# Gate and up projections as Strassen products of 2x2 blocks, the down projection with tokens stationary, and the first expert steps among the last attention pairs

## The chip, the cores and the metric

The kernel runs on one core of one Trainium2 chip. The metric is the device time of one execution in microseconds (us), the median of several runs. A core has five engines with an instruction stream each: TensorE (PE; its weight loads are listed apart as PEld), Vector (DVE), Scalar (ACT), GpSimd (POOL) and Sync (SP, which here issues all DMAs). They wait for each other by semaphores only. TensorE reads SBUF and writes PSUM; Vector and Scalar read both; GpSimd works on SBUF.

## What is computed

One transformer block on `x` (16 batches, 112 tokens, 256 channels: 1792 tokens). First cross attention to a context of 375 tokens per batch, then a mixture of 8 experts, each applied to every token, and summed with weights from two softmaxes over the experts:

```python
x = x + _L0_xattn_ref(_layernorm(x), ctx_1024, Wq, bq, Wk, bk, Wv, bv)
x = x + _L0_ffn_ref(_layernorm(x), w_router, w_gating, w_gate, w_up, w_down)
# ffn, with E, F = 8, 1024 and GATE_TEMP = 0.1
router_probs = softmax(x @ w_router); gate_weights = softmax(x @ w_gating / 0.1)
h = silu(einsum('bsh,ehf->ebsf', x, w_gate)) * einsum('bsh,ehf->ebsf', x, w_up)
expert_out = einsum('ebsf,efh->ebsh', h, w_down)
cw = router_probs * gate_weights; cw = cw / (sum(cw) + 1e-9)
out = einsum('ebsh,bse->bsh', expert_out, cw)
```

All is float32. The kernel reaches that with the faster matmul type fp32r in three passes: each operand is split into a high part (the value rounded to fp32r) and a low part (the value less the high part), and a product is high x high + high x low + low x high.

## The kernel before

**Streams.** Each engine's program is written out by hand, in order, in its own block (`@block.sync` L252, `gpsimd` L328, `scalar` L440, `vector` L633, `tensor` L902). An engine does its instructions in that order only; `wait_ge` on a semaphore holds everything behind it.

**Attention.** Batches go in 8 pairs of two. A pair is a chain through the engines: normalise (Scalar, `norm1`), transpose (TensorE), split into high (Scalar) and low parts (Vector), queries, scores, maxima (Vector, `maxima` L666), exponentials (Scalar), transposes of the probabilities, mix, values, residual, second layer norm (`stats2` L700 on Vector, `norm2_terms` L353 on GpSimd, `norm2` L448 on Scalar), transpose, router logits. Parts of neighbouring pairs are interleaved; `pair` in each block writes the order down. GpSimd makes the low part of the context (`low_ctx` L358, which on the profile's page shows as w_lo from shared, since the tiles overlap) and adds the value bias (`add_bv` L365). The transposed, normalised rows are split into `st_hi`, `st_lo` and copied by DMA into the SBUF tiles `h_in_hi`, `h_in_lo` (`keep_input` L276).

**Experts.** An expert's F = 1024 goes in two halves, a half in 4 tiles of 128 columns, the tokens in 4 chunks of 448. One step s (32 per expert) is one tile and one chunk. `gate_up` (L1074) makes 12 matmuls: weights (128 x 128) are the stationary side, 448 tokens the moving side, 2 slices of the 256 channels, 3 passes, for gate and for up. Scalar does Silu (`activate` L514), Vector multiplies with up (`hidden` L713, at L719), Scalar makes the high part (L522), Vector the low part (through `low`, L238). `down` (L1100) comes 2 steps later (LAG): 6 matmuls of 448 tokens, with the 128 x 128 tiles of `w_down` stationary. After 4 steps Vector multiplies the result with the combine weights, which lie along the tokens and were spread over the partitions by a DMA from DRAM (L871), and GpSimd adds it to `acc` (L420). At the end `acc` is transposed back (`sum_rows` L1142) and added to x. Weights come by DMA, half by half; Scalar makes high parts (L511), GpSimd low parts (L378).

**Overlap of the stages.** The first 8 steps of expert 0 lie among the last attention chain (from `pair` 7 on) by hand. Loops: the middle attention pairs and experts 1 to 6 are hardware loops. All matmuls of three passes are recorded at L233, inside `accumulate`.

Of the kernel before, what the change touches and what calls it, by code (L numbers as in the profile page):

```python
# [5 lines left out]
def xattn_ffn_kernel(nc, x, ctx, wq, bq, wk, bk, wv, bv, w_router, w_gating, w_gate, w_up, w_down, out):  # L16
# [3 lines left out]
    B, TQ, D = x.shape  # L20
# [10 lines left out]
    CH = 4  # L31
    TC = T // CH
    BC = B // CH
    HALVES = 2
    FH = F // HALVES
    FT = FH // P
    STEPS = HALVES * CH * FT
    LAG = 2
    HS = 4
    EARLY = 2 * FT  # L40
# [4 lines left out]

    x_v = x.rearrange("b q d -> q b d")
    out_v = out.rearrange("b q d -> q b d")
    ctx_v = ctx.rearrange("(n two) (p t) d -> n p two (t d)", two=2, t=KT)
    gate_v = w_gate.rearrange("e (k p) (h f) -> e h p k f", p=P, h=HALVES)
    up_v = w_up.rearrange("e (k p) (h f) -> e h p k f", p=P, h=HALVES)  # L50
    down_v = w_down.rearrange("e (h t p) d -> e h p t d", p=P, h=HALVES)
    cw_dram = nc.dram_tensor("cw_dram", (E, T), fp32).ap()

    es = ExitStack()
    with es:
# [6 lines left out]
        def at_least(engine, semaphore, count):  # L62

            if not isinstance(count, int) or count > 0:
                engine.wait_ge(semaphore, count)

# [14 lines left out]
        m_hi = sb("m_hi", [P, DK, D], fp32r)  # L81
        m_lo = sb("m_lo", [P, DK, D], fp32r)
        wv_hi = sb("wv_hi", [P, DK, D], fp32r)
        wv_lo = sb("wv_lo", [P, DK, D], fp32r)
        wr_raw = sb("wr_raw", [P, DK, 2 * E])
        wr_split = sb("wr_split", [P, DK, 2, 2 * E], fp32r)
        wr_hi, wr_lo = wr_split[:, :, 0, :], wr_split[:, :, 1, :]

        xs = sb("xs", [TQ, B, D])
        h_in_hi = sb("h_in_hi", [P, DK, T], fp32r)  # L90
        h_in_lo = sb("h_in_lo", [P, DK, T], fp32r)
        w_raw = sb("w_raw", [P, 3, DK * FH])
        w_hi = sb("w_hi", [P, HALVES, 3, DK * FH], fp32r)
        w_lo = sb("w_lo", [P, HALVES, 3, DK * FH], fp32r)


        cn_hi, cn_lo = [w[0:KP, HALVES - 1, :, :].rearrange("p a n -> p (a n)")[:, 0:4 * KT * D]
                        .rearrange("p (s b t d) -> p s b t d", s=2, b=2, t=KT) for w in (w_hi, w_lo)]
        ct_hi = sb("ct_hi", [P, 2, DK, SK], fp32r)
        ct_lo = sb("ct_lo", [P, 2, DK, SK], fp32r)  # L100
        shared = sb("shared", [P, 4 * KT * D])
        ctx_raw = shared[0:KP, :].rearrange("p (s b n) -> p s b n", s=2, b=2)
        xt_hi = sb("xt_hi", [P, DK, TP], fp32r)
# [119 lines left out]
        def inside(p):  # L223

            return not isinstance(p, int) or 0 <= p < PAIRS
# [1008 lines left out]
```

## Time and profile before

| | us |
|---|---|
| median of 3 runs | 1077.63 |
| lowest, highest | 1076.79, 1095.28 |
| span of the profiled execution | 1092.8 |
| TensorE busy in it | 1066.6 |
| Vector, Scalar, GpSimd busy | 515.0, 420.8, 315.2 |

The profile is of one execution, which took 1.4% longer than the median of the runs. Lines such as L233 are lines of the kernel. A row of the timeline gives start and duration in us; neighbouring instructions of one kind are merged (x6). "[2.41 <-DMA ...]" is the idle time of the engine before it and what ended it. A matmul's duration covers its way through the array, so matmuls overlap and what one costs is the distance between two starts.

### The profile page before, as it was taken

What the parts mean: (1) busy time and instruction counts of PE and PEld (TensorE: products, weight loads), DVE (VectorE), ACT (ScalarE), POOL (GpSimd) and SP (SyncE); (2) the same over time, 40 slices, a digit from 0 to 9 for tenths busy, and PEclk for the clock granted to TensorE, in tenths of its full rate; (3) what the DMA queues carried; (4) which work ended last, traced back from release to release, by engine and by line L of the source; (5) the groups of instructions that cost most, each with busy time, mean ns of one, the idle gap of its engine ahead of it and who ended that gap; (6) DMA issues with size and microseconds to landing.
All of it is one profiled execution on the core that took longest, in us unless ns stands there. A gap on an engine that the chain in (4) does not pass through costs nothing.

```text
span 1092.8 us, 14974 instructions
## 1 busy us (share of the span) xinstructions
PE 1066.6 (98%) x5457; PEld 975.0 (89%) x5457; DVE 515.0 (47%) x832; ACT 420.8 (39%) x787; POOL 315.2 (29%) x247
## 2 busy tenths in 40 slices
PE   6798999999999999999999999999999999999998
PEld 5688999999999999999999999999999999999997
DVE  5777754434444343434443444434344444344444
ACT  3677644424342332434243424333243434243322
POOL 3554403304132131414141413213141413141110
PEclk8899999999999999999999999999999999999999
DMA  7223212100102010101010010201010201000001
GB/s 178 94 79 99 96 37 92 62 14 18 57 1 75 17 58 0 66 17 66 0 53 21 17 58 0 74 13 61 0 66 17 66 0 44 31 17 1 1 17 51
DMA packets 34086, 47.38 MB, mean 43 GB/s; under 512 B 3016, under 2 KB 23864, under 8 KB 34056
## 3 DMA queue, kind: packets, MB, share of 16 engines
q1 hardware_dynamic: 34056, 46.97, 13.6%
q8 instruction: 19, 0.31, 0.1%
q14 instruction: 11, 0.09, 0.0%
HBM read 41.40 MB, written 1.89 MB: 40 GB/s over the span
## 4 chain that ended last, share of the span: by engine, by line
PE 91%; DMA 3%; DVE 2%; POOL 1%; issue 1%; ACT 1%; SPq 0%; DVEq 0%; POOLq 0%
PE ps L233 89%; DMA shared<-in_ctx 3%; POOL w_lo L362 1%; DVE part L662 0%; POOL rstd L347 0%; DVE neg_top L676 0%; PE ps L1150 0%; PE ps L997 0%; PE ps L920 0%; PE ps L946 0%; POOL xs L370 0%; DVE top L669 0%; DVE top_all L674 0%; DVE bn L637 0%; PE ps L991 0%
## 5 line engine op out<-in xcount | busy, mean ns | idle before, releaser
L233 PE MATMUL ps<-h_in_hi,w_hi 128*128 128x448 f32 x1024 | 377.4, 369 | 0.0
L233 PE MATMUL ps<-h_in_lo,w_hi 128*128 128x448 f32 x1024 | 376.7, 368 | 0.0
L233 PE MATMUL ps<-h_in_hi,w_lo 128*128 128x448 f32 x1024 | 375.5, 367 | 0.0
L719 DVE TENSOR_TENSOR hid<-act,ps 128x448 f32<-128x448 f32 x256 | 159.0, 621 | 365.3 <-PE ps L233 294.3
L420 POOL TENSOR_TENSOR acc<-acc,part 128x896 f32<-128x896 f32 x59 | 125.1, 2121 | 636.8 <-DVE part L871 636.8
L233 PE MATMUL ps<-hs,w_hi 128*128 128x448 f32 x1008 | 288.2, 366 | 0.0
L522 ACT CAST hs<-hid 128x448 fp32r<-128x448 f32 x256 | 145.2, 567 | 348.4 <-DVE hid L719 348.4
L238 DVE TENSOR_TENSOR hs<-hid,hs 128x448 fp32r<-128x448 f32 x256 | 185.6, 725 | 162.1 <-ACT hs L522 162.1
L519 ACT ACTIVATE act<-ps 128x448 f32<-128x448 f32 x256 | 139.6, 545 | 260.5 <-PE ps L233 260.3
L233 PEld LDWEIGHTS ps<-h_in_hi,w_lo 128*128 128x128 f32 x1024 | 192.3, 188 | 19.0
L233 PEld LDWEIGHTS ps<-h_in_hi,w_hi 128*128 128x128 f32 x1024 | 192.4, 188 | 18.8
L233 PEld LDWEIGHTS ps<-h_in_lo,w_hi 128*128 128x128 f32 x1024 | 192.1, 188 | 17.7
L233 PEld LDWEIGHTS ps<-hs,w_hi 128*128 128x128 f32 x1008 | 188.6, 187 | 19.4 <-issue 0.2
L233 PE MATMUL ps<-hs,w_lo 128*128 128x448 f32 x504 | 185.1, 367 | 0.0
L378 POOL TENSOR_TENSOR w_lo<-w_raw,w_hi 128x512 fp32r<-128x512 f32 x96 | 132.6, 1413 | 53.6 <-ACT w_hi L511 53.6
L233 PEld LDWEIGHTS ps<-hs,w_lo 128*128 128x128 f32 x504 | 94.3, 187 | 8.5
L871 DVE TENSOR_TENSOR part<-ps,shared 128x896 f32<-128x896 f32 x59 | 64.0, 1084 | 0.0
L511 ACT CAST w_hi<-w_raw 128x512 fp32r<-128x512 f32 x96 | 51.7, 618 | 0.0
L362 POOL TENSOR_TENSOR w_lo<-shared,w_hi 125x768 fp32r<-125x768 f32 (+1 forms) x16 | 29.0, 1835 | 3.7 <-ACT w_hi L502 3.4
L920 PE MATMUL ps<-ident,shared 125*128 125x125 f32 x96 | 15.1, 300 | 10.0 <-DMA shared<-in_ctx 10.0
L920 PEld LDWEIGHTS ps<-ident,shared 125*128 125x128 f32 x96 | 12.3, 156 | 11.9 <-issue 6.2
L345 POOL TENSOR_TENSOR var<-mv,eps_c 112x2 f32<-112x2 f32 (+2 forms) x12 | 2.4, 198 | 67.1 <-DVE mv L706 52.7
(140 smaller groups left out, 582.8 us busy)
## 6 DMA issues: line engine op xcount, KB each, us to landing
w_raw<-in_L_ffn_w_gate SPq DMA_DIRECT2D x16, 512.0 KB, 3.6
w_raw<-in_L_ffn_w_up SPq DMA_DIRECT2D x16, 512.0 KB, 4.7
w_raw<-in_L_ffn_w_down SPq DMA_DIRECT2D x16, 512.0 KB, 5.6
shared<-cw_dram SPq DMA_DIRECT2D x32, 224.0 KB, 3.2
shared<-in_ctx SPq DMA_DIRECT2D x8, 750.0 KB
h_in_hi<-st_hi SPq DMA_DIRECT2D x8, 224.0 KB, 3.0
h_in_lo<-st_lo SPq DMA_DIRECT2D x8, 224.0 KB, 3.4
out_dram<-xs SPq DMA_DIRECT2D x3, 448.0 KB, 3.2
```

Of the source, the lines that this page charges most:

```text
L233: ins = nc.tensor.matmul(dst, w, m, start=first and i == 0, stop=last and i == len(passes) - 1)
L238: return nc.vector.tensor_tensor(dst, src, high.bitcast(fp32), ALU.subtract)
L345: nc.gpsimd.tensor_tensor(var, mv[:, :, 1], eps_c[:, 0:n], ALU.add).then_inc(norm_step, 1)
L362: nc.gpsimd.tensor_tensor(cn_lo[:, bass.ds(p % 2, 1), b, :, :], ctx_raw[:, bass.ds(p % 2, 1), b, :].rearrange("p s (t d) -> p s t d", t=KT ...
L378: ins = nc.gpsimd.tensor_tensor(w_lo[:, half, i, s], w_raw[:, i, s], w_hi[:, half, i, s].bitcast(fp32), ALU.subtract)
L420: nc.gpsimd.tensor_tensor(a, a, part[:, c % 2, :, :], ALU.add).then_inc(acc_done, 1)
L511: ins = nc.scalar.copy(w_hi[:, half, i, s], w_raw[:, i, s])
L519: nc.scalar.activation(act[:, s % 2, :], ps_g[s % 2], ACT.Silu).then_inc(act_done, 1)
L522: nc.scalar.copy(hs[:, 0, s % HS, :], hid[:, s % 2, :]).then_inc(hid_hi_done, 1)
L719: nc.vector.tensor_tensor(hid[:, s % 2, :], act[:, s % 2, :], ps_u[s % 2], ALU.mult).then_inc(hid_done, 1)
L871: nc.vector.tensor_tensor(dst, ps_d[c % 2], cw_all[:, None, c * TC:(c + 1) * TC].broadcast_to((P, DK, TC)), ALU.mult).then_inc(part_done, 1)
L920: ins = nc.tensor.transpose(ps_c[:, k, t * KP:(t + 1) * KP], ctx_raw[:, slot, b, at:at + P], ident[0:KP, 0:KP])
```

## The change

**Strassen products.** Tokens go in two halves (CP = 2) of 896, each in two chunks of TC = 448. A *quad* is two neighbouring tiles of F, the two slices of the 256 channels, and the two chunks of a half: a product of 2x2 blocks by 2x2 blocks. It needed 8 block products and takes 7, from sums of the input blocks (`xc`, made once per token half) and of the weight blocks. The 64 quads n cover everything; two quads (FPAIRS) make a *group* g, the half of an expert's F for one token half. Each of the 7 products is three passes, as before:

```diff
+    PRODUCTS = {1: (A11, B11), 2: (A12, B21), 3: (S4, B22), 4: (A22, T4), 5: (S1, T1), 6: (S2, T2), 7: (S3, T3)}
+            def product(n, m, p, bank, first):
+                cp, fp = n // FPAIRS % CP, n % FPAIRS
+                a, b = PRODUCTS[p]
+                return accumulate(bank, three(w_hi[:, fp, m, b, :], w_lo[:, fp, m, b, :], xc_hi[:, cp, a, :], xc_lo[:, cp, a, :]),
+                                  first=first, onto=not first)
+            def gate_2_7(n):
+                pe.wait_ge(gate_p1, n + 1)
+                product(n, 0, 2, g_a, False).then_inc(gate_prod, 1)
+                pe.wait_ge(gate_sum, 5 * n + U2_SUM)
+                product(n, 0, 7, g_x, False).then_inc(gate_prod, 1)
```

`gate_1_6_5` starts three PSUM banks, `gate_2_7` adds products 2 and 7 onto two of them, `gate_4_3` products 4 and 3; the same for up. Between them Scalar copies product 1 out (`gate_first`, `up_first`) and Vector makes five sums for gate and five for up, each from PSUM and an SBUF tile, in place:

```diff
+            def gate_first(n):
+                at_least(sc, hid_done, 4 * (n - 1) + HID21)
+                first_product(n, gate_prod, g21, g_a, gate_p1)
+            def up_first(n):
+                at_least(sc, hid_lo_done, 4 * (n - 1) + HID21)
+                first_product(n, up_prod, u21, u_a, up_p1)
+            def up_u2(n):
+                ve.wait_ge(up_p1, n + 1)
+                ve.wait_ge(up_prod, 7 * n + PROD[6])
+                at_least(ve, hid_lo_done, 4 * n)
+                nc.vector.tensor_tensor(u12, u_x, u21, ALU.add).then_inc(up_sum, 1)
```

Each tile is there once. The four hidden blocks of a quad (`hidden11`, `22`, `21`, `12`) are products of Silu(gate) and up; only `hidden11` reads PSUM, the other three read two SBUF tiles. Scalar makes their high parts (`high_hidden`), GpSimd their low parts, which Vector did before.

**Weights.** A *set* is gate and up for one pair of tiles. GpSimd makes four sums of 128 x 256 (`sums_of_set`), Scalar one high copy of 128 x 1792 (`high_set`), GpSimd one low part of 128 x 1792 (`low_set`); `w_down` is split in one piece of 1024 columns (`high_down`, `low_down`).

**Down with tokens stationary.** For each group and each of its 7 token tiles of 128, 12 matmuls with the hidden tokens as the stationary side and 256 channels moving. The result lies with tokens on partitions, so the combine weight is a number per partition and one Vector instruction scales and adds it (`add_rows`). No broadcast of `cw` by DMA, no `acc` addition on GpSimd, no `sum_rows`. The rows after attention go to DRAM (`keep_x1`) and come back as 14 tiles of 128 tokens, which is the accumulator.

```diff
+            def row_passes(g, i, fp):
+                return [t for j in range(2) for t in three(h[:, 0, j, toks], h[:, 1, j, toks],
+                                                           w[:, 0, 2 * fp + 1 - j, :], w[:, 1, 2 * fp + 1 - j, :])]
+            def add_rows(g, i, src):
+                nc.vector.scalar_tensor_tensor(acc[:, tile, :], src, cw[:, tile, e:e + 1], acc[:, tile, :],
+                                               ALU.mult, ALU.add).then_inc(acc_done, 1)
```

**The order** of the steady stretch, on TensorE, Vector, Scalar and GpSimd:

```diff
+            def quad(n):
+                g = n // FPAIRS - 1
+                gate_1_6_5(n)
+                if n % FPAIRS:
+                    down(g, 4)
+                up_1_6_5(n)
+                if n % FPAIRS:
+                    down(g, 5)
+                gate_2_7(n)
+                up_2_7(n)
+                down(g, 6 if n % FPAIRS else 0)
+                gate_4_3(n)
+                if n % FPAIRS == 0:
+                    down(g, 1)
+                up_4_3(n)
+                if n % FPAIRS == 0:
+                    down(g, 2)
+                    down(g, 3)
...
+                if n > 1:
+                    gate_u2(n)
+                    if odd:
+                        add_rows(g, 2, ps_r[2])
+                        add_rows(g, 3, ps_r[3])
+                    up_u2(n)
+                gate_u3_c22(n)
+                if n > 1 and odd:
+                    add_rows(g, 4, ps_r[4])
+                    add_rows(g, 5, ps_r[5])
+                up_u3_c22(n)
...
+                if n > 1 and odd:
+                    add_rows(g, 6, ps_r[6])
+                gate_c21_c12(n)
+                hidden11(n)
+                if n > 1 and not odd:
+                    add_rows(g, 0, ps_r[0])
+                    add_rows(g, 1, ps_r[1])
+                hidden22(n)
+                up_c21(n)
+                up_c12(n)
+                hidden21(n)
+                hidden12(n)
...
+                    gate_first(n)
+                    high_hidden(n - 1, HID21, u21, 0, TC)
+                    high_hidden(n - 1, HID12, u12, 1, 0)
+                    up_first(n)
...
+                    low_hidden(n - 1, HID21, u21, 0, TC)
+                    low_hidden(n - 1, HID12, u12, 1, 0)
...
+                low_hidden(n, HID11, g11, 0, 0)
+                low_hidden(n, HID22, u22, 1, TC)
```

Scalar's `high_set` comes after `up_first` in the first and last of four quads; GpSimd's `low_set`, `sums_of_set` and `low_down` come between its two pairs of low parts.

**The first steps.** Quads 0 and 1 lie among the last attention pairs. The input sums of token half 0 are made in pairs 6 and 7 (Vector `sums_1_3`, `sums_2_4`; Scalar `high_comb`; GpSimd `low_comb`), those of half 1 after the last pair:

```diff
+            last = PAIRS - 1
+            transpose_probs(last, 0)
+            transpose_probs(last, 1)
+            gate_4_3(0)
+            mix_ctx(last)
+            up_1_6_5(0)
+            transpose_mix(last)
+            up_2_7(0)
+            values(last)
+            transpose_norm2(last - 1)
+            up_4_3(0)
+            gate_1_6_5(1)
+            transpose_norm2(last)
+            up_1_6_5(1)
+            route(1)
+            gate_2_7(1)
+            up_2_7(1)
+            gate_4_3(1)
+            up_4_3(1)
```

The router is two plain float32 matmuls for each of 14 token tiles, in two calls (`route(0)` in pair 6, `route(1)` above), instead of split ones for each pair. The weight split of sets 0 and 1 lies in pairs 1 to 4. Nothing is a hardware loop any more: every instruction is written out.

## Rows read from the trace of the kernel before

**Rows 1.** The page, busy us (share of the span) and instructions of each engine
```profile
PE 1066.6 (98%) x5457; PEld 975.0 (89%) x5457; DVE 515.0 (47%) x832; ACT 420.8 (39%) x787; POOL 315.2 (29%) x247
```
**Rows 2.** The chain that ended last in order of time: start, us, what
```profile
161.78 879.73 PE ps L233 x4272
1041.51 0.87 PE ps L1150 x8
```
**Rows 3.** Groups by line: out<-in, shapes, count | busy us, mean ns | idle before, releaser
```profile
L238 DVE TENSOR_TENSOR hs<-hid,hs 128x448 fp32r<-128x448 f32 x256 | 185.6, 725 | 162.1 <-ACT hs L522 162.1
L719 DVE TENSOR_TENSOR hid<-act,ps 128x448 f32<-128x448 f32 x256 | 159.0, 621 | 365.3 <-PE ps L233 294.3 <-ACT act L519 70.9
...
L378 POOL TENSOR_TENSOR w_lo<-w_raw,w_hi 128x512 fp32r<-128x512 f32 x96 | 132.6, 1413 | 53.6 <-ACT w_hi L511 53.6
L420 POOL TENSOR_TENSOR acc<-acc,part 128x896 f32<-128x896 f32 x59 | 125.1, 2121 | 636.8 <-DVE part L871 636.8
...
L519 ACT ACT_TABLE_LOAD x2 | 2.6, 1283 | 0.0
```
**Rows 4.** Timeline of PE: start us, us, what; same matmul, one expert step apart
```profile
603.96 0.37 PE L233 MATMUL ps<-h_in_hi,w_hi 128*128 128x448 f32 x1
...
607.67 0.37 PE L233 MATMUL ps<-h_in_hi,w_hi 128*128 128x448 f32 x1
```
**Rows 5.** Timeline and chain: first and last of 18, of 10; router; plain fp32
```profile
137.62 0.28 PE L233 MATMUL ps<-w_hi,pt_hi 125*112 125x256 f32 x1
...
139.63 0.28 PE L233 MATMUL ps<-w_hi,pt_lo 125*112 125x256 f32 x1
...
104.92 0.28 PE L233 MATMUL ps<-xt_hi,m_lo 128*128 128x224 f32 x1
...
105.93 0.27 PE L233 MATMUL ps<-xt_hi,m_lo 128*128 128x224 f32 x1
...
107.83 0.09 PE ps L991
...
37.16 3.55 PE L997 MATMUL ps<-lg 112*112 112x256 f32 x8
```
**Rows 6.** Windows: length, busy of PE, PEld, DVE, ACT, POOL, clock, DMA, GB/s
```profile
120.00:140.00 20.00, 19.98 (x134) 18.78 (x134) 13.78 (x28) 11.72 (x24) 4.91 (x6) 1.00 0.12 40
...
200.00:620.00 420.00, 420.00 (x2041) 382.56 (x2040) 182.57 (x255) 150.37 (x275) 118.09 (x71) 1.00 0.11 35
```
**Rows 7.** Timeline of DVE and POOL, alone and beside each other
```profile
129.06 0.62 DVE L238 TENSOR_TENSOR at_lo<-ps,at_hi 128x448 fp32r<-128x448 f32 x1 [2.01 <-ACT at_hi L489]
129.60 0.61 DVE L238 TENSOR_TENSOR st_lo<-ps,st_hi 128x448 fp32r<-128x448 f32 x1
...
43.63 3.79 POOL L378 TENSOR_TENSOR w_lo<-w_raw,w_hi 128x512 fp32r<-128x512 f32 x3 [7.69 <-ACT w_hi L511]
...
123.12 3.66 POOL L362 TENSOR_TENSOR w_lo<-shared,w_hi 125x768 fp32r<-125x768 f32 x2
...
123.84 2.95 DVE L674 SCALAR_TENSOR_TENSOR top_all<-q_bk,c,top 112x2 f32<-112x2 f32 x1
...
619.23 8.30 POOL L378 TENSOR_TENSOR w_lo<-w_raw,w_hi 128x512 fp32r<-128x512 f32 x6
```
**Rows 8.** Timeline of PE after three idles, and the window of 40 to 60
```profile
53.38 0.34 PE L233 MATMUL ps<-wv_hi,at_hi 128*112 128x256 f32 x1 [4.27 <-DVE at_lo L238]
...
72.21 0.86 PE L920 MATMUL ps<-ident,shared 125*128 125x125 f32 x6 [2.41 <-DMA shared<-in_ctx]
...
73.08 0.33 PE L233 MATMUL ps<-ct_lo,q_hi 128*112 128x376 f32 x1
...
97.77 0.85 PE L920 MATMUL ps<-ident,shared 125*128 125x125 f32 x6 [2.21 <-DMA shared<-in_ctx]
...
98.72 0.52 PE L233 MATMUL ps<-ct_lo,q_hi 128*112 128x376 f32 x1
...
40.00:60.00 20.00, 15.44 (x107) 14.71 (x107) 16.86 (x42) 13.07 (x27) 11.40 (x13) 0.90 0.12 44
```

More of the change, by code:

```diff
@@ new lines, in xattn_ffn_kernel @@
+        ctx_raw = shared[0:KP, 0:4 * KT * D].rearrange("p (s b n) -> p s b n", s=2, b=2)
+        gate_t = shared[:, 0:4 * TC].rearrange("p (s t) -> p s t", s=4)
+        up_t = shared[:, 4 * TC:7 * TC].rearrange("p (s t) -> p s t", s=3)
+        g21, g12, g22, g11 = [gate_t[:, i, :] for i in range(4)]
+        u21, u12, u22 = [up_t[:, i, :] for i in range(3)]
+        CT, PT, CN = 2 * DK * SK, 2 * KT * TQ, 4 * KT * D
+        sizes = [CT, CT] + [DK * TP] * 6 + [DK * D] * 4 + [PT, PT, CN, CN]
+        starts = [sum(sizes[:i]) for i in range(len(sizes) + 1)]
@@ L434, in _ @@
-            expert(0, first=True)
-            with pool.Fori(1, E - 1) as e:
-                expert(e)
-            expert(E - 1, last=True)
+            low_set(0)
+            pair(3)
+            sums_of_set(1)
+            pair(4)
+            low_set(1)
+            pair(5)
+            low_comb(0, COMB_SPLITS[0:3])
+            pair(6)
+            low_comb(0, COMB_SPLITS[3:4])
+            pair(7)
+            norm2_terms(6)
+            low_hidden(0, HID11, g11, 0, 0)
+            low_hidden(0, HID22, u22, 1, TC)
@@ L440, in _ @@
+            for n in range(1, QUADS):
+                quad(n)
+            low_hidden(QUADS - 1, HID21, u21, 0, TC)
+            low_hidden(QUADS - 1, HID12, u12, 1, 0)
         @block.scalar
@@ L633, in _ @@
+            for n in range(1, QUADS):
+                quad(n)
+            high_hidden(QUADS - 1, HID21, u21, 0, TC)
+            high_hidden(QUADS - 1, HID12, u12, 1, 0)
         @block.vector
@@ L828, in _ @@
+            stats2(last)
+            hidden22(0)
+            up_c21(0)
+            hidden21(0)
+            up_c12(0)
+            hidden12(0)
+            sums_1_3(1)
+            gate_u2(1)
+            up_u2(1)
+            sums_2_4(1)
+            keep_logits(1)
+            lv = logits[:, :, :].rearrange("p i (two e) -> p (i two) e", two=2)
+            ve.wait_ge(logits_done, CP)
             nc.vector.tensor_reduce(lg_top[:], lv, AX.X, ALU.max).then_inc(cw_step, 1)
             ve.wait_ge(cw_step, 1)
-            nc.vector.tensor_tensor(lg[:], lv, lg_top[:, :, None].broadcast_to((TQ, 2 * B, E)), ALU.subtract).then_inc(cw_step, 1)
@@ L902, in _ @@
+            for n in range(1, QUADS):
+                quad(n)
+            for i in range(RT):
+                add_rows(GROUPS - 1, i, ps_end[i])
         @block.tensor
@@ new lines, in _ @@
+            for n in range(2, QUADS):
+                quad(n)
+            g = GROUPS - 1
+            pe.wait_ge(wd_done, SETS)
+            pe.wait_ge(hid_lo_done, 4 * (QUADS - 1))
+            pe.wait_ge(acc_done, RT * g)
+            pe.wait_ge(act_done, 4 * (QUADS - 1) + HID11)
+            pe.wait_ge(gate_sum, 5 * QUADS)
+            for i in range(RT):
+                accumulate(ps_end[i], row_passes(g, i, 0), first=i % 2 == 0, last=False)
+            pe.wait_ge(hid_lo_done, 4 * QUADS)
```

995 lines of the change are left out of this document (491 added, 504 removed).

## The prediction

> **What bounds the kernel now.** I read the page's busy row first [rows 1], then the chain of work that ended last [rows 2], then the groups by line [rows 3]. TensorE is busy for 1066.6 of 1092.8 us. One piece of the chain, from 161.8 to 1041.5 us, is matmuls of L233 and nothing else: 880 us in which TensorE waits for nobody. Before it the attention pairs take about 121 us, with some TensorE waits, and after it come 51 us more of the same with four transposes of sums. Vector is idle for 365 us before L719 alone, and GpSimd for 637 us before L420 [rows 3]. So a matmul taken away is worth its own spacing, as long as nothing else becomes late.
>
> A matmul lasts 0.37 us and overlaps the next, so the price is the distance of starts: 18 matmuls of 448 columns in 3.71 us, 0.206 each [rows 4]. With 256 columns it is 17 in 2.01 us, 0.118 each [rows 5]. There the stationary side has 112 columns and after the change 128; 224 columns with 128 stationary ones come every 0.112 [rows 5], so the wider load is hidden under 0.118.
>
> **What TensorE does less.** Before: 8 experts x 32 steps x 18 = 4608 matmuls of 448 columns, 949 us. After: 64 quads (two 128-column tiles of F by 896 tokens) x 2 x 7 products x 3 passes = 2688 of 448 columns, 553.5 us, and 32 groups x 7 token tiles x 12 = 2688 of 256 columns, 317 us. Sum 870.5. Gain 78.5. The down projection has the same columns as before; all of the gain is the eighth of gate and up. The four `sum_rows` go, 0.87 each, 3.5 [rows 2]. The router turns from 64 fp32r matmuls of 0.09 (L991, [rows 5]) into 28 of plain fp32. Bounds: 0.09 each, and 0.42 each (8 of 256 columns in 3.55 us, [rows 5]); that is -3.5 to +5.5. I take 0.21 a piece, no change. The x1 round trip over DRAM, the `cw` broadcasts that go, and the smaller weight loads lie under TensorE work: DMA engines are 11% busy there [rows 6]. SP issues the accumulator load behind `load_down(0)` and `load_set(2)`, after the last `transpose_norm2`; Vector first needs it in quad 2, some 20 us later. If it is late, `add_rows` and all sums queued behind it on Vector wait (the start rival below).
>
> **What the other engines do more, for one group (two quads, 84 + 84 matmuls, 27.2 us of TensorE).** Vector: 28 operations of 448 columns (20 sums, 8 products) and 7 row additions. One begins 0.54 after the one before it (129.06, 129.60, [rows 7]), a row addition between 0.31 (by its 256 columns) and 0.54, and I take 0.4: 18 us. Scalar: 20 copies or Silus of 0.57 and its part of the splits, about 14. GpSimd: 3 pieces of 512 took 3.79 us [rows 7], one of 896 2.12 [rows 3], so 2.2 ns a column: 448 columns 1.12, 1792 columns 4.1, and with 8 low parts, a `low_set`, a `sums_of_set` and half a `low_down` 17 us a group, against 7.6 us in as much time now (118 of 420, [rows 6]). None is over 27, so no engine becomes the bound by its sum. The question is the order, since each product waits for a sum on Vector, and the tiles g21, u21, u12 hold both the next first product and the last hidden block.
>
> Laid beside each other, with t=0 at gate P1 of an even quad: the gate P7 of the odd quad before landed at -4.9 (18 products, 3.7, and down 6, 1.4, follow it, less 0.16 of landing). Vector then has 10 operations of 0.54, two waits of 0.12 for its own result and 3 rows of 0.4: `hidden21` begins at 1.9 and is done at 2.6. Scalar makes the gate's P1 copy first, then the high part: 3.7. GpSimd does `low21` to 4.8 and `low12` to 5.95. The U2 sum of up waits for all four low parts (`hid_lo_done`): 6.0 to 6.6. TensorE can start up P7 at 6.7; 27 matmuls of 0.206 bring it there at 5.56. **Late by 1.2 us, once a group.** Late next would be gate P7 by 0.1. In odd quads the two downs of 1.4 each in between cover the same chain, and in the last part of an even quad downs 1 to 3 do. I take 1.3 x 31 groups = 40.
>
> Here a shared thing matters. Vector operations with two SBUF inputs stretch while GpSimd works, and those that read PSUM don't: two elements took 2.95 us at 123.84, when GpSimd had begun two pieces at 123.12 that ended at 126.78; the low parts of L238 take 725 ns in the mean [rows 3] against 620 for the PSUM kind [rows 7]. `hidden22`, `hidden21`, `hidden12` and the input sums are of that kind. But the handover overlaps: 6 GpSimd pieces took 8.30 us at 619 [rows 7] against 6 x 1.26 = 7.58; three low parts of L238 fall among them (one in each step of 3.71), 0.24 for each and not 0.62. My 1.2 counts it so. Counted in full, `low22` starts only behind `hidden12` (3.4), the low parts end at 6.75 and P7 starts at 7.5: 2.0 late.
>
> The Trainium skill (SBUF — State Buffer, "SBUF: two separate sides") calls this pair of ports an exclusive lock that the first of the two holds for its whole instruction, while the other fully blocks. By that rule the sum would be 22 us higher than mine; the rows at 619 to 628 bear out the blocking, and speak for less than the whole instruction.
>
> **Where the first steps lie.** TensorE hardly waits in the last pairs now: 19.98 of 20 us busy from 120 to 140 [rows 6]. The same layout from pair 6 on, with the durations of [rows 3, 7], gives these waits after the change. (a) In pair 6 GpSimd gets three pieces of `low_comb` (2.1 + 1.1 + 2.1) ahead of `norm2_terms(4)`, and they wait for Scalar's copies; `transpose_norm2(4)` comes 3.2 late. (b) Eight short ones in pairs 6 and 7 (a comb part 1.1, the copy of P1 behind two exponentials 1.3, others under 0.8): 5.3. (c) `gate_4_3(0)` waits for U3 behind residual, statistics and two low parts on Vector: 2.1; up P7(0): 1.4. (d) `transpose_norm2(7)`: statistics are done late, and `norm2_terms(7)` is queued on GpSimd behind a low part: 4.3. (e) `gate_4_3(1)`: Vector stands in `sums_2_4(1)` until GpSimd has `low_comb` done, and `gate_u3_c22(1)` is queued behind it: 4.7. (f) Quad 2 waits for Scalar's two table loads (1283 ns, [rows 3]) and for the combine weights on Vector: 5.5. Sum 26.5. Bounds: 12, if (d) and (e) shrink to the short ones; 35, if (a) and (e) meet GpSimd at its loaded rate. Before pair 6 the weight split moves (7.6 us of GpSimd go, 13.8 come, some late); TensorE waited 4.3 us up to 53.4 for it, and 2.2 up to 97.8 for a context load [rows 8]. I take 0, bounds -4 to +4.
>
> After both idles matmuls were slower for a while: one of 376 columns lasted 0.52 at 98.7 and not 0.33 as at 73.1; the granted clock over 40 to 60 us is 0.90 [rows 5, 8], which is 4 us of the 20 at 1.2 GHz and not 2.4, most of them at work: about 1.6 us lost each time. (a), (d) and (e) are as long: 5.
>
> **The sum:** 1092.8 - 78.5 - 3.5 + 40 + 26.5 + 5 + 0 = 1082. The profiled execution is 1.4% over the median shown (1077.63), so 1082 x 0.986 = 1067. The saving shrinks with a faster execution while the waits on Vector and GpSimd do not, so I say **1068**.
>
> **Rivals.**
> - *The chain stays hidden* (20%). If sums, copies and low parts answer as fast as matmuls need them, only the start costs: 1042, so about 1027. For it: Vector 18 of 27 us, Scalar 14 of 27. Against it: the layout above, with starts of 0.54 that several rows show.
> - *GpSimd's row is the loop, the other sign* (20%). One mechanism: the low parts. At the port held in full it is 2.0 a group: 1103, so 1088. If GpSimd works at its present mean (512 columns in 1413 ns, not 1263, [rows 3]) and Vector misses its turn as at 123.84 [rows 7], the low parts grow by 12%, at each of four and at the 4.1 us piece, and a group is 2.9 late: 1131, so 1115. It is slower than before from 1.65 a group, by over 2% from 2.35.
> - *The clock falls in the steady stretch* (8%). An idle of 1.2 to 2.0 us once a group; 2.4 us up to 72.2 were not followed by slower matmuls (376 columns in 0.33 at 73.1), 2.2 up to 97.8 were (0.52 at 98.7) [rows 8]. 31 x 1.6 = 50 more: 1132, so 1116.
> - *A start far worse than laid out* (5%): weights or the accumulator land late, GpSimd stands in `sums_of_set`: +25, 1092.
> - The forecast: 47%, its own range 1048 to 1088.
>
> **How the numbers follow.** "Within 2%" is 1056 to 1099, about what a measurement of this kernel can tell from no change. Faster: the first rival, and the fifth of the forecast under 1056, 0.30. Slower: half of the second, the clock, and a little of the start, 0.21. Same: 0.49. The range leaves out the lower half of the first rival and the upper ends of second and third: 1032 to 1108.
>
> **What would show it.** Spacing 0.206 and 0.118 in the steady stretch, or the term 78.5 is wrong. A wait of TensorE in L233 of 1.2 to 2 us in total once in about 28.5 us, ended by Vector or Scalar, and none in odd quads; a period of 27.2 is the first rival. `hidden` operations of two SBUF inputs over 0.62 in the mean, sums with PSUM at 0.62. Waits of 3 to 5 us near 120, 160 and 173 us. The granted clock at 1.00 from 190 us on. GpSimd busy at about 60%. The prediction is wrong if Vector or GpSimd has a larger sum than 18 and 17 us a group, or if the waits before quad 3 sum to under 10.

## The result, and the profile after

The changed kernel takes 1100.24 us (median of 4 runs, 1099.99 to 1101.56) against 1077.21 us for the kernel before: a ratio of 1.0219, 95% interval 1.0199 to 1.0239. It is slower by 23 us (the interval leaves open whether by more or less than 2%), where I forecast 1068 with a range of 1032 to 1108. One thing has to be said to read the numbers: the kernel before has executions of two lengths, about 1077 and about 1096 us, and the profile shown above is of one of the long ones; the ratio is against the short ones.

The page of the changed kernel, busy us of each engine, against [rows 1]:

```profile
PE 1021.7 (93%) x6160; PEld 941.5 (86%) x6160; DVE 789.0 (72%) x1361; ACT 499.1 (45%) x874; POOL 643.7 (59%) x532
```

TensorE is busy 45 us less than before, and the span is 7 us longer. So 52 us of idle have come. Its windows (length, busy of PE, PEld, DVE, ACT, POOL, granted clock, DMA) show that they lie in two places. Up to 194 us, where quad 2 has just begun, it is idle for 44 us at a clock of 0.83; in the steady stretch it is idle for 6.6 us in 200:

```profile
0.00:194.00 194.00, 150.03 (x878) 138.05 (x879) 126.32 (x268) 106.19 (x207) 98.05 (x121) 0.83 0.27 82
...
200.00:400.00 200.00, 193.41 (x1171) 178.15 (x1169) 146.72 (x243) 89.55 (x151) 123.90 (x92) 1.00 0.10 30
```

**The steady stretch.** The chain of waits, one group (28.8 us) like the next; this is the turn from an odd to an even quad, and gate P1 of the even quad starts at 393.47:

```profile
395.34 0.81 DVE shared L856
...
396.17 0.02 ACT shared L567
...
396.60 0.58 ACT arena L594
...
397.25 2.51 POOL arena L411 x2
...
399.87 0.64 DVE shared L827
...
400.55 1.46 PE ps L248 x8
```

It is the chain of the forecast, link by link: `hidden21` (L856), Scalar's copy of gate P1 (L567), the high part (L594), `low21` and `low12` (L411), the U2 sum of up (L827), up P7. TensorE's timeline over it (start, us, the idle before it and what ended it):

```profile
397.52 0.36 PE L248 MATMUL ps<-xc_hi,w_lo 128*128 128x448 f32 x1
398.45 0.47 PE L248 MATMUL ps<-xc_hi,w_hi 128*128 128x448 f32 x1 [0.57 <-DVE shared L807]
398.76 0.36 PE L248 MATMUL ps<-xc_lo,w_hi 128*128 128x448 f32 x1
...
400.55 0.47 PE L248 MATMUL ps<-xc_hi,w_hi 128*128 128x448 f32 x1 [0.43 <-DVE shared L827]
```

The idle shown is 0.57 and 0.43, but by starts gate P7 comes 0.73 later than a spacing of 0.2, up P7 0.59, and the first matmul behind each pause takes 0.31 to the next and not 0.20. Together it is 1.75 us a group; 84 matmuls at 0.2027 and 84 at 0.1196 (12 in 1.44) make 27.07, and the period is 28.82.

**The start.** TensorE's longer waits, against 2.4 us and less after 55 us in [rows 8]:

```profile
88.38 1.01 PE L1099 MATMUL ps<-ident,early 112*128 112x112 f32 x4 [2.40 <-ACT early L489]
...
125.54 1.01 PE L1099 MATMUL ps<-ident,early 112*128 112x112 f32 x4 [3.48 <-ACT early L489]
...
170.80 1.01 PE L1099 MATMUL ps<-ident,early 112*128 112x112 f32 x4 [4.60 <-ACT early L489]
...
187.36 0.44 PE L248 MATMUL ps<-xc_hi,w_hi 128*128 128x448 f32 x1 [0.18 <-ACT shared L583]
...
191.32 0.74 PE L248 MATMUL ps<-xc_hi,w_hi 128*128 128x448 f32 x1 [3.11 <-DVE shared L819]
```

The last two rows are gate P1 and gate P6 of quad 2. P6 goes to a PSUM bank that a gate sum of quad 1 reads, and waits for all of them; the last two (L817, L819) stand on Vector behind the combine weights, which end at 190.2. In experiments 4 and 12 I took this wait for one before gate P3 of quad 1. That product starts at 185.19, without a wait.

The first of the waits, at 88.38, is one that I had not laid out. L1099 is `transpose_norm2`. It waits for Scalar's `norm2`, that for GpSimd's `norm2_terms(2)`, and GpSimd stood in `sums_of_set(1)` in front of it, since the weights were late (timeline of GpSimd):

```profile
82.76 0.74 POOL L390 TENSOR_TENSOR w_raw<-w_raw 128x256 f32<-128x256 f32 x1 [9.63 <-DMA w_raw<-in_L_ffn_w_up]
```

SP issues `load_set(1)` behind `load_ctx(5)`, which waits for the low part of pair 3's context; so its two DMAs were issued at 72.3 and 72.8, and the second landed at 82.7.

### The profile page after: what moved, and what is told of

It reads as the page before. It is cut to its first block, busy times and chain, and to the rows that moved or that the text cites. A ratio compares the mean times of both kernels' runs of the same rounds, so it can differ in the third digit from the quotient of the medians.

```text
span 1099.8 us, 16297 instructions
## 1 busy us (share of the span) xinstructions
PE 1021.7 (93%) x6160; PEld 941.5 (86%) x6160; DVE 789.0 (72%) x1361; ACT 499.1 (45%) x874; POOL 643.7 (59%) x532
## 4 chain that ended last, share of the span: by engine, by line
PE 53%; DVE 24%; POOL 10%; issue 4%; ACT 4%; DMA 4%; DVEq 0%; SPq 0%; POOLq 0%; ACTq 0%
PE ps L248 51%; POOL arena L411 7%; DVE xsacc L867 3%; DMA shared<-in_ctx 3%; DVE shared L856 2%; DVE shared L811 2%; DVE shared L833 2%; DVE shared L827 2%; DVE shared L813 2%; DVE shared L819 2%; ACT arena L594 2%; DVE shared L831 2%; DVE shared L846 2%; DVE shared L851 2%; DVE shared L837 1%
## 5 line engine op out<-in xcount | busy, mean ns | idle before, releaser
L411 POOL TENSOR_TENSOR arena<-shared,arena 128x448 fp32r<-128x448 f32 x256 | 311.7, 1233 | 309.1 <-ACT arena L594 306.2
L248 PE MATMUL ps<-arena 128*128 128x256 f32 (+4 forms) x3120 | 425.3, 289 | 7.8 <-DVE arena L252 5.5
L248 PEld LDWEIGHTS ps<-arena 128*128 128x128 f32 (+2 forms) x3120 | 414.4, 194 | 15.0 <-DVE arena L252 4.5
L248 PE MATMUL ps<-xc_hi,w_hi 128*128 128x448 f32 x896 | 342.0, 382 | 38.0 <-DVE shared L807 17.1
L248 PE MATMUL ps<-xc_lo,w_hi 128*128 128x448 f32 x896 | 329.8, 368 | 0.0
L248 PE MATMUL ps<-xc_hi,w_lo 128*128 128x448 f32 x896 | 329.8, 368 | 0.0
L248 PEld LDWEIGHTS ps<-xc_hi,w_hi 128*128 128x128 f32 x896 | 170.9, 191 | 80.3 <-DVE shared L807 28.2
L248 PEld LDWEIGHTS ps<-xc_hi,w_lo 128*128 128x128 f32 x896 | 170.3, 190 | 14.4
L248 PEld LDWEIGHTS ps<-xc_lo,w_hi 128*128 128x128 f32 x896 | 171.2, 191 | 9.0
L594 ACT CAST arena<-shared 128x448 fp32r<-128x448 f32 x256 | 141.1, 567 | 75.6 <-DVE shared L851 55.4
L567 ACT COPY shared<-ps 128x448 f32<-128x448 f32 x128 | 68.3, 533 | 172.4 <-PE ps L248 121.5
L827 DVE TENSOR_TENSOR shared<-ps,shared 128x448 f32<-128x448 f32 x64 | 40.0, 624 | 105.1 <-ACT shared L567 59.2
L867 DVE SCALAR_TENSOR_TENSOR xsacc<-ps,cw,xsacc 128x256 f32<-128x256 f32 x224 | 98.6, 476 | 13.8 <-PE ps L248 13.8
L861 DVE TENSOR_TENSOR shared<-shared 128x448 f32<-128x448 f32 x64 | 70.2, 1097 | 0.1
L856 DVE TENSOR_TENSOR shared<-shared 128x448 f32<-128x448 f32 x64 | 67.3, 1051 | 0.1
L851 DVE TENSOR_TENSOR shared<-shared 128x448 f32<-128x448 f32 x64 | 58.7, 917 | 0.0
```

What stands on the lines that cost most here:

```text
L248: ins = nc.tensor.matmul(dst, w, m, start=first and i == 0, stop=last and i == len(passes) - 1, skip_group_check=onto)
L411: nc.gpsimd.tensor_tensor(h[:, 1, j, at:at + TC], tile, h[:, 0, j, at:at + TC].bitcast(fp32), ALU.subtract).then_inc(hid_lo_done, 1)
L567: nc.scalar.copy(dst, bank).then_inc(done, 1)
L594: nc.scalar.copy(hs[n % HSLOTS][:, 0, j, at:at + TC], tile).then_inc(hid_hi_done, 1)
L827: nc.vector.tensor_tensor(u12, u_x, u21, ALU.add).then_inc(up_sum, 1)
L851: nc.vector.tensor_tensor(u22, g22, u22, ALU.mult).then_inc(hid_done, 1)
```

## The experiments

Experiments 5 and 9 look at the kernel before again; all others are edits of the changed kernel (1100.2 us). They were made in three groups. The kernel before, beside them, took 1077.03 us in the first four, 1077.74 in the next four and 1079.02 in the last four (medians of its short executions), so a difference of 1 to 2 us between two groups says nothing.

**1. Work of TensorE in front of the two late products.** The half of the first four row tiles that needs only the earlier quad's hidden blocks comes ahead of gate P7.

```diff
+            def down_early(g, some):
+                for i in some:
...
+                    accumulate(ps_r[i], row_passes(g, i, 0), first=i % 2 == 0, last=False)
...
                     down(g, 4)
+                else:
+                    down_early(g, (0, 1))
                 up_1_6_5(n)
...
                     down(g, 5)
+                else:
+                    down_early(g, (2, 3))
                 gate_2_7(n)
```

> The changed kernel with one thing moved: in every even quad, the 6 matmuls of each of the first four row tiles whose stationary side is the hidden block of the earlier quad of the group (24 matmuls of 256 columns, 2.87 us) come before gate P7, the other 6 of each stay where they were. Nothing else is moved. Theory A (in an even quad TensorE waits only because gate P7 and up P7 come before Vector and GpSimd have closed the last quad, 1.75 us a group): the need for both comes 2.87 us later, the waits of 0.6 and 0.4 us at gate P7 and up P7 vanish, a group goes from 28.8 to about 27.1 us, and the time falls by about 53, to 1047 us. Theory B (Vector and GpSimd go round in a loop of their own that is as long as 28.8 us): the wait comes back later in the same quad, which has 12 matmuls less behind its P7 products, and the time stays within 10 us of 1100.

Measured: 1047.27 us (ratio 0.9729, 0.9712 to 0.9745), 53 us less, as theory A had it. The chain of waits of this kernel has one piece from 300 us on:

```profile
299.88 724.70 PE ps L248 x4500
```

So Vector and GpSimd have no loop of their own of 28.8 us. They were late by a fixed amount in even quads, and 2.9 us of work in front of the need covers it.

**2. A second set of tiles.** g21, g12, u21, u12 of odd quads lie elsewhere, and the waits on their low parts go back by one quad.

```diff
-                at_least(sc, hid_lo_done, 4 * (n - 1) + HID21)
-                first_product(n, up_prod, u21, u_a, up_p1)
+                at_least(sc, hid_lo_done, 4 * (n - 2 if n > 2 else n - 1) + HID21)
+                first_product(n, up_prod, buf(n, U21), u_a, up_p1)
```

> The changed kernel with a second set of the tiles g21, g12, u21, u12 for odd quads (in the tile of the input sums, which is free by then). A first product or a U2 sum then waits for no high or low part of the quad before; only Vector's own queue is left. Theory A (the low parts hold up P7: hidden21, Scalar, two low parts, U2): the wait before up P7 vanishes, the one before gate P7, which hangs on Vector being through with hidden12, stays at 0.6 to 0.9; 0.9 us a group less, 28 us in all: 1072 us. Rival (the port is held by four low parts in a row, and Vector's own ten operations are what comes late): the wait moves and no more than 8 us are gained, 1092 or more.

Measured: 1064.79 us (0.9886, 0.9870 to 0.9903), 35 us less where 28 were expected and the rival allowed 8. TensorE has no wait before up P7 any more and one of 0.36 before gate P7. About 1.15 of the 1.75 us were the reuse of a tile; the rest is at gate P7, which waits for Vector's U2 sum of gate.

**3. GpSimd's order in the attention pairs.**

```diff
             pair(3)
-            sums_of_set(1)
             pair(4)
-            low_set(1)
+            sums_of_set(1)
             pair(5)
-            low_comb(0, COMB_SPLITS[0:3])
+            low_set(1)
```

In pairs 6 and 7 the low parts of the input sums follow `norm2_terms`.

> The changed kernel with GpSimd's order in pairs 3 to 7 changed alone: the sums of weight set 1 come after the work of pair 4 instead of ahead of it, the low part of set 1 after pair 5, and the low parts of the input sums after the terms of the second layer norm in pairs 6 and 7 instead of ahead of them. Theory A (the lost time before quad 2 is instructions that stand in GpSimd's queue, waiting for a DMA or for Scalar, ahead of norm2_terms): TensorE's waits of 2.4 us at 88 and 3.5 us at 125 vanish, the granted clock between 80 and 140 us rises from 0.83 to over 0.9, and the time falls by 8 to 14 us, to about 1090. Rival (the context's DMA and Scalar's longer queue set the pairs): 3 us or less.

Measured: 1093.41 us (1.0155, 1.0138 to 1.0172), 6.8 us less; the waits at 88 and 125 are gone and the clock from 60 to 100 us is 1.00 (0.91 and 0.83 in the changed kernel). From 100 to 140 us it is 0.83 (0.91 and 0.83), and there waits of 4.9 and 4.2 us came up before `values`, where Vector is late. One reason for the first is in the timeline of Vector and GpSimd:

```profile
95.20 1.24 POOL L373 TENSOR_TENSOR xsacc<-xsacc,early 112x256 f32<-112x256 f32 x2
95.30 5.09 DVE L759 SCALAR_TENSOR_TENSOR neg_top<-q_bk,c,top_all 112x2 f32<-112x2 f32 x1
...
96.39 3.98 POOL L400 TENSOR_TENSOR w_lo<-w_raw,w_hi 128x1792 fp32r<-128x1792 f32 x1
```

A Vector operation on two elements a partition, from two SBUF inputs, takes 5.09 us, until GpSimd has ended two short instructions and the long low part of a weight set. The exponentials, queries and scores of the pair hang on it.

**4. Matmuls for nothing in the waits.**

```diff
+            def fill_wait(n):
+                for _ in range(n):
+                    nc.tensor.matmul(ps[0:TQ, 7, 448:512], ident[:, 0:TQ], ident[:, 0:64], start=True, stop=True)
```

> The changed kernel with matmuls whose result nobody reads, put where TensorE waits: 16 before transpose_norm2(4) (a wait of 3.5 us), 20 before transpose_norm2(7) (4.6 us), 14 before gate P3 of quad 1 (3.1 us). Each is plain fp32 of 64 columns. No wait is removed. Theory A (a good part of what the start costs is not the waits but the slow matmuls after them, at granted clocks of 0.74 to 0.75 from 140 to 200 us): the clock there rises and the time falls by 4 to 10 us. Rival (the slow matmuls lie beside waits for other engines and cost nothing themselves): the time stays within 2 us, or rises by as much as the dummies overshoot.

Measured: 1100.89 us (1.0222, 1.0200 to 1.0244): no change. The window of 160 to 180 us of the changed kernel, and then of this one:

```profile
160.00:180.00 20.00, 14.92 (x72) 13.91 (x72) 12.23 (x20) 7.90 (x15) 11.03 (x11) 0.75 0.37 119
```

```profile
160.00:180.00 20.00, 18.66 (x126) 17.30 (x124) 13.11 (x19) 7.11 (x13) 12.37 (x11) 0.91 0.45 144
```

The clock rose from 0.75 to 0.91. Behind the router TensorE was 5.7 us earlier than in the changed kernel (175.14 against 180.82), and half of that was waited away at gate P4 of quad 1, for Vector:

```profile
182.19 0.51 PE L248 MATMUL ps<-xc_hi,w_hi 128*128 128x448 f32 x1 [2.81 <-DVE shared L811]
```

So at the end of the attention most of the slow matmuls lie beside Vector's queue, as the rival has it. But 2.4 us were left (182.19 against 184.59), and the experiment does not say what they are worth: the third group of matmuls stood before gate P3 of quad 1, where the changed kernel has no wait, and took 5.1 us. In the steady stretch TensorE was 1.1 us earlier than in the changed kernel (224.48 against 225.54 for the first gate P7 that waits), which the times of the two kernels don't tell apart.

**5 and 9. The kernel before, profiled again.**

> The kernel before, unchanged, for a second profile. In the profile of 1092.8 us matmuls of 448 columns are 0.2059 us apart for most of the steady stretch; in the changed kernel and its variants they are 0.2027 apart, with and without waits. Theory A (the 1.4% between that execution and the median is this spacing, so it belongs to the execution and not to the kernel, and must not be taken off the changed kernel's sum): an execution of about 1077 shows 0.2025 to 0.203 throughout. Rival (the spacing is a property of the kernel, as its matmuls follow each other without a break; the 16 us lie in the attention pairs): 0.2059 again, and the pairs are shorter.

> The kernel before, unchanged, once more: the second profile was again of an execution of 1097 us, with 448 columns 0.2059 apart, and of 7 executions beside it 4 took 1077.7 to 1078.1 and 3 took 1096 to 1097. If this profile is of an execution of about 1077: Theory A (the two times are two matmul spacings) expects 0.2023 to 0.203 through the steady stretch, 4608 matmuls by 0.0035 being the 16 us; the rival expects 0.2059 and the difference elsewhere. If it is of 1096 again, nothing is told apart.

The first of these executions took 1097.34 us and showed 0.2059 again. The second took 1077.10. Its chain has the piece of [rows 2] with the same 4272 matmuls, 862.34 us and not 879.73:

```profile
162.08 862.34 PE ps L233 x4272
```

That is 0.2019 a matmul and not 0.2059; the 17.4 us are nearly all of the 17.7 between the two spans (1075.1 and 1092.8), and up to 162 us the two agree within 0.3. Theory A holds. The changed kernel's own matmuls are 0.2027 apart in its profile. Why an execution takes one spacing or the other stays open; the granted clock is 1.00 in both.

**6. The first two quads behind the attention.** Quads 0 and 1 begin when the last pair is through, on all engines.

```diff
-            gate_4_3(0)
             mix_ctx(last)
-            up_1_6_5(0)
             transpose_mix(last)
-            up_2_7(0)
             values(last)
...
+            route(1)
+            gate_1_6_5(0)
+            up_1_6_5(0)
```

> The changed kernel with quads 0 and 1 taken out of the last attention pairs: the last pair's attention runs to its end, then quad 0 begins. The steady stretch is untouched. Theory A (the quads among the last pairs fill waits that the attention chain has anyway): the chain of the last pair then stands open, some 10 to 15 us of waits come, and the 17 us of work of quads 0 and 1 lie behind it: 1110 to 1120 us. Rival (the quads themselves make the waits, through Scalar's and GpSimd's queues, as in transpose_norm2(7) behind a low part): the time stays within 5 us of 1100.

Measured: 1114.05 us (1.0335, 1.0311 to 1.0358), 14 us more. Theory A: that part of the change is worth having, since the waits of the attention chain are there with or without the quads. `transpose_norm2(7)` waits 4.7 us here too.

**7. Short pieces.** Experiment 3, with the low parts of sets 0 and 1 in 4 instructions each.

> The kernel with GpSimd's order changed (1093.4 us), and in it the low parts of weight sets 0 and 1, which lie among the attention pairs, in 4 pieces of 384 and 512 columns each instead of one of 1792 (3.98 us). There a Vector operation of two elements took 5.09 us beside it. Theory A (Vector waits for the end of a GpSimd instruction, so long instructions hurt its short ones): that operation takes 1 to 2.5 us, and the time falls by 2 to 4 us, to 1090. Rival (Vector gets no turn between GpSimd's pieces either): no change, within 1 us.

Measured: 1094.98 us (1.0161, 1.0138 to 1.0184), which is no gain. The same small operation of Vector still takes 4.56 us, over two short GpSimd instructions and three of the four pieces:

```profile
100.20 4.56 DVE L766 SCALAR_TENSOR_TENSOR neg_top<-q_bk,c,top_all 112x2 f32<-112x2 f32 x1
...
100.11 1.24 POOL L373 TENSOR_TENSOR xsacc<-xsacc,early 112x256 f32<-112x256 f32 x2
101.30 4.39 POOL L403 TENSOR_TENSOR w_lo<-w_raw,w_hi 128x512 fp32r<-128x512 f32 x4
```

No gain, as the rival has it: between GpSimd instructions that follow each other at once, Vector got no turn at about 101.3, 102.4 and 103.5, and one at 104.6. It is not so each time. In experiment 3, beside three pieces that follow each other as closely, two such operations took 1.07 and 1.05 us:

```profile
111.71 1.07 DVE L757 SCALAR_TENSOR_TENSOR top_all<-q_bk,c,top 112x2 f32<-112x2 f32 x1
112.82 1.05 DVE L759 SCALAR_TENSOR_TENSOR neg_top<-q_bk,c,top_all 112x2 f32<-112x2 f32 x1
...
110.64 5.24 POOL L380 TENSOR_TENSOR xc_lo<-xf,xc_hi 128x896 fp32r<-128x896 f32 x3 [1.78 <-ACT xc_hi L551]
```

By the lengths of these pieces (2.1 and 1.1 us) each operation ended about where a piece did, near 112.7 and 113.8. What decides between the two cases stays open.

**8. All of it together,** with Vector's `sums_2_4(0)` behind `at_low(5)`.

> The changed kernel with the row matmuls moved, the second set of tiles, GpSimd's order and the short pieces all together, and Vector's second pair of input sums after at_low of pair 5 instead of ahead of it. The parts that act on different stretches should add: 1047.3 less 6.8 (GpSimd's order), less 2 to 4 (pieces), less 2 to 4 (the wait of 4.2 us before values(5), where Vector stood in the sums): 1032 to 1037 us. The second tiles add nothing, as no wait is left for them. Rival (the waits of the start only move): 1040 or more.

Measured: 1039.95 us (0.9652, 0.9630 to 0.9674). Against experiment 1 that is 7.3 less, which is GpSimd's order alone (6.8); the pieces and Vector's order added nothing that can be told. Closer to the rival. That the waits of the start only moved, as it says, was not tried part by part.

**10 and 11. One more GpSimd operation of 448 columns ahead of `low21`,** in odd quads, then in even quads.

```diff
                 if n > 1:
+                    if n > 2 and n % 2 == 1:    # == 0 in experiment 11
+                        pool.wait_ge(hid_hi_done, 4 * (n - 1) + HID21)
+                        nc.gpsimd.tensor_tensor(xf[:, 0, :], u21, hs[(n - 1) % HSLOTS][:, 0, 0, TC:2 * TC].bitcast(fp32), ALU.subtract)
                     low_hidden(n - 1, HID21, u21, 0, TC)
```

> The changed kernel with one more GpSimd operation of 448 columns (1.25 us) ahead of low21 in every odd quad from 3 on, whose result nobody reads. In an odd quad two row tiles (2.9 us) lie before gate P7, and the U2 sum of up is done 3.1 us before up P7 needs it. Theory A (the low-part chain is late in even quads only): within 3 us of 1100. Rival (GpSimd's total, 58% busy and holding the port, is what slows the loop): +15 to +37 us.

> The same additional GpSimd operation, but in every even quad from 4 on, 30 in all. Theory A (in even quads hidden21, Scalar, low21, low12, U2, up P7 is the path): each delays up P7 by its own 1.25 us, 30 x 1.25 = 37: about 1137 us. Rival (the wait at gate P7, which hangs on Vector's queue, sets the quad, and up P7 merely follows): less than 15 us.

Measured: 1099.45 us in odd quads (1.0191, 1.0154 to 1.0227), and 1155.71 in even quads (1.0707, 1.0654 to 1.0760). So the chain decides in even quads only, as laid out. But there it costs 55 us, not 37: 1.8 us for each 1.25. TensorE now waits already at up P2, for Scalar's copy of up P1, which waits for `low21`. The timeline of TensorE in the kernel with the even ones has the rest:

```profile
716.38 0.47 PE L248 MATMUL ps<-xc_hi,w_hi 128*128 128x448 f32 x1 [0.56 <-DVE shared L810]
...
718.28 0.69 PE L248 MATMUL ps<-xc_hi,w_hi 128*128 128x448 f32 x1 [1.02 <-ACT shared L570]
718.77 0.57 PE L248 MATMUL ps<-xc_lo,w_hi 128*128 128x448 f32 x1
719.14 0.57 PE L248 MATMUL ps<-xc_hi,w_lo 128*128 128x448 f32 x1
```

Behind the second wait matmuls start 0.37 to 0.54 apart and not 0.20. This is so from up P7 on in 22 of the 30 groups, and in 8 it isn't, at the same two waits. From one such group to the next it is 29.9 us where the matmuls keep their pace, 1.1 more than in the changed kernel: that is the chain. It is 31.0 to 31.2 where they don't: the slow matmuls take another 1.1 to 1.3. Windows of 50 us show a clock of 0.93 to 1.00 there, and 1.00 in the changed kernel:

```profile
550.00:600.00 50.00, 46.37 (x257) 41.81 (x256) 33.95 (x56) 21.17 (x35) 30.88 (x23) 0.93 0.07 22
```

This is the third rival of the forecast, at a wait of 1.02 us behind one of 0.56 instead of 0.43 behind 0.57.

**12. The end of the attention.** Experiment 8, with `norm2_terms(7)` ahead of `low_hidden(0, HID22, ...)`, `transpose_norm2(last)` behind `up_1_6_5(1)`, and `combine_weights()` behind `hidden12(1)`.

> The kernel with all changes together (1040.0 us) and three orders more at the end of the attention: norm2_terms(7) on GpSimd ahead of the low part of hidden22 of quad 0, transpose_norm2(7) on TensorE behind the first three up products of quad 1, and Vector's combine weights behind hidden12 of quad 1 instead of ahead of its gate sums. Theory A (the waits of 4.6 us at transpose_norm2(7) and 3.1 us at gate P3 of quad 1 are these queues): the first falls to 1 or less (1.6 us sooner, 1.8 to 2.7 us of products ahead of it), the second to under 1; 5 to 7 us less: 1033 to 1035. Rival (Vector's sums and the input sums of the second token half, in the same queue, are the path there): 2 us or less.

Measured: 1036.85 us (0.9608, 0.9566 to 0.9649), 3.1 less than experiment 8, between the two theories. By the ratios to the kernel before it would be 4.7. The wait at `transpose_norm2(7)` is gone, and the one of 3.1 us at gate P6 of quad 2; in their place TensorE waits 3.4 us at 175 for the U3 sum of quad 1's gate, behind Vector's input sums of the second token half. From 189 us its chain is TensorE alone, up to 1016:

```profile
189.03 827.34 PE ps L252 x5133
```

This is the fastest version, 40 to 42 us under the kernel before: of the 64 us that matmul starts and the 3.5 that `sum_rows` give (see below), some 40 are left once the waits of the steady stretch are covered.

## Why the prediction was wrong, point by point

I forecast -9.6 us against the median, and it was +23. Three terms of the sum failed, all to the same side: the price of a matmul that goes (13 us), the wait once a group (15 us) and the start (8 us). By terms, in the order of the sum; the measured ones are between the profiled executions of 1075.1 and 1099.8 us, which are 24.7 apart:

| term | forecast (x 0.986) | measured |
|---|---|---|
| matmul starts | -77.4 | -64.0 |
| `sum_rows` | -3.5 | -3.5 |
| wait once a group | +39.4 | +54.2 |
| waits of the start | +26 | +21 |
| slow matmuls of the start | +5 | about +18 |
| sum | -10.5 | about +26 |

**Matmul starts: the price was wrong, not the count.** Before, 4608 x 0.2019 = 930.4; after, 2688 x 0.2027 + 2688 x 0.1196 = 866.4. I took 0.206 from [rows 4], a row of the long execution. Against an execution of 1077 us the 1920 matmuls of 448 columns that go are worth 0.2019 each: 8 us of the error. Another 2 come from 0.2027 for those that stay, and 4 from 0.1196 and not 0.118 for those of 256 columns. The factor 0.986 gave back one of them. The 1.4% between the profiled execution and the median was the spacing of the 448-column matmuls in the expert stretch, and not a stretch of all that the kernel does, so it had to be taken off by their counts, 4608 before and 2688 after. In all 13 us. That the distance of starts prices a matmul, and that 128 stationary columns are hidden under 256 moving ones, was right. By the same prices gate and up give 75 us, and the down projection with tokens stationary costs TensorE 11 more than before (321.5 for 1536 x 0.2019 = 310.1), where I had taken the two as equal.

**The wait once a group: the right chain, sized too low, 15 us.** The links, from gate P1 of the even quad: `hidden21` begins at 1.87 (forecast 1.9), its high part is done at 3.71 (3.7), `low12` at 6.29 (5.95), U2 at 7.04 (6.6), up P7 starts at 7.08 (6.7). The part that was off is the low parts: 1.25 each in the chain (mean of the group 1.233), where I had taken 1.12, the length of such a piece when it runs alone. They are 0.26 of the 0.38 by which up P7 starts later than laid out. TensorE also comes to it 0.09 sooner, with matmuls 0.2027 apart, and the first matmul behind the pause loses 0.1. Gate P7 was late by 0.73 and not by 0.1, since `hidden12` takes 1.57 us beside GpSimd; up P7 waits that much less for it, and this and the restarts before it don't add to the sum. The means of the products with two SBUF inputs say how much Vector stretches beside GpSimd:

```profile
L861 DVE TENSOR_TENSOR shared<-shared 128x448 f32<-128x448 f32 x64 | 70.2, 1097 | 0.1
L856 DVE TENSOR_TENSOR shared<-shared 128x448 f32<-128x448 f32 x64 | 67.3, 1051 | 0.1
L851 DVE TENSOR_TENSOR shared<-shared 128x448 f32<-128x448 f32 x64 | 58.7, 917 | 0.0
L807 DVE TENSOR_TENSOR shared<-ps,shared 128x448 f32<-128x448 f32 x64 | 40.0, 625 | 24.4 <-ACT shared L567 20.3
```

0.92 to 1.10 us, against 0.62 with an input in PSUM; before it was 0.725 [rows 3]. The second rival came nearest, at 20%: its sign and its mechanism, slower low parts, which was about half of the excess. But 1.75 lies only just above its break-even of 1.65 and under both of its prices, 2.0 and 2.9; 1.75 in my sum, with all else as forecast, would have given 1082 us, and not 1100. With the right price of a matmul the break-even would have been 1.2, not 1.65, and my own 1.3 would have been above it.

**The start: the waits a little less, the slow matmuls more than three times as much.** TensorE is idle for 44 us up to 194, against 23 up to 160 in the profile of 1075.1 us. Forecast waits (a) 3.2 and (d) 4.3 measured 3.5 and 4.6; (c) measured 1.9 and 1.2 for 2.1 and 1.4; (e) did not come: gate P4 and P3 of quad 1 follow without a wait. Of the 5.5 of (f) came 3.1, for the combine weights in Vector's queue, and 0.2 behind Scalar's table loads. What I put at 0 did come: between 60 and 120 us, ahead of all the waits that I had laid out, TensorE is idle for 13.5 us, and for 6.1 in the profile of 1075.1 us. The 2.4 at 88.38 are the moved weight split. I had counted the GpSimd time of the split (13.8 for 7.6) and not that `load_set(1)` is queued behind a wait of SP, and `norm2_terms` behind it. Experiment 3 prices this at 6.8 us together with (a). The other waits of this stretch are for context loads (0.9 to 1.9 us) and for low parts of Vector (2.0 and 2.2); no experiment took them apart. The clock is 0.83 over 194 us against 0.91 over 160, here in the profile of 1075.1 us:

```profile
0.00:160.00 160.00, 137.16 (x910) 128.19 (x911) 106.85 (x256) 96.63 (x198) 65.73 (x98) 0.91 0.34 99
```

That is 66 us at 1.2 GHz against 29, most of them at work. Without the matmuls of experts, at their full-clock price (94 after, 118 before), TensorE is busy for 131 us against 113; this is the +18. The router's second half shows it (chain; 28 entries are 14 matmuls, and the first half took 3.20 at 118.86):

```profile
175.19 5.79 PE ps L1108 x28
```

At the full clock that is 0.23 a matmul; all 28 would be 6.4 us against 5.8 for the 64 small ones (0.09 each), about as taken. But experiment 4 says that the clock is not a term to be added freely: where Vector is nearly as late as TensorE, a faster TensorE gains little. I can't give its share of the +18 on the path; that stays open, and so does how the 39 us of the start divide beyond the 10 that experiments 3 and 12 took away.

**The rivals.** Chain hidden: refuted as the change is written, and true of experiment 1. GpSimd's row is the loop: not the loop (experiments 1 and 10), but the chain through it (2 and 11). Port held for the whole instruction: it was 22 us on my sum, for a group that is 2.0 late, and the group was 1.75 late, between the two. The Trainium skill (SBUF — State Buffer, "SBUF: two separate sides") speaks of a lock held for an instruction; two rows, of experiments 3 and 7, show more than that, a Vector operation held over several GpSimd instructions in a row, and `hidden21` in the steady stretch shows less (0.80 us at 395.34, while GpSimd makes low parts of 1.2 us from 394.50 on). The clock falls in the steady stretch: not behind waits of 0.57 and 0.43 us, but behind 0.56 and 1.02 in most groups (experiment 11). Range and side: 1100 lies inside the range, and the sign was wrong. That it lies inside is no merit of the sum; the range was drawn wide for the rivals.

## What to carry to other kernels

Look at more than one execution before pricing the unit that the gain is made of: a spacing of 0.2059 or 0.2019 us was 17 us of 1077, and a ratio of medians must not be laid on a kernel whose terms don't share it. A chain that is late by a fixed time once per turn is mended with the bottleneck engine's own work that doesn't hang on the chain (53 us here, from 24 matmuls moved), or by a second tile where the reuse of one makes the link (35 us). And when a step is moved past a wait in a queue that only issues, follow what is queued behind its first use: here a late load stopped GpSimd, and with it the next pair's norm.

## What the hardware showed that I had not expected

- The same program runs with 448 columns every 0.2059 or every 0.2019 us over 880 us, at a granted clock of 1.00 in both.
- GpSimd instructions that follow each other without a gap can keep a Vector operation with two SBUF inputs out over several of them: 5.09 us for two elements, and 4.56 with the long instruction cut in four. Beside another such run it took 1.05 us.
- Behind a wait of 1.0 us that follows one of 0.56, TensorE ran at half its pace for some matmuls of the steady stretch in 22 of 30 groups, and behind 0.43 in none that I read; 1.25 us more in the chain cost 1.8.
